# A graph network's sort of edges into slots: one of its three table operations goes from VectorE to GpSimd, and the scatter of edge weights is placed behind the sort

## The reference, cut to what matters

```python
def _L0_gnn_ref(feat, edge_src, edge_dst):
    deg = jax.ops.segment_sum(jnp.ones_like(edge_dst, dtype=feat.dtype), edge_dst, num_segments=n)
    norm = jnp.power(jnp.clip(deg, 1.0, None), -0.5)[:, None]
    for _ in range(10):
        msg = h[edge_src] * norm[edge_src]
        agg = jax.ops.segment_sum(msg, edge_dst, num_segments=n)
        h = 0.9 * (agg * norm) + 0.1 * feat_0
...
h = relu(layernorm(x)); x = x + _L0(h, src, dst)
h = relu(layernorm(x)); x = x + _L1(h, src, dst, q, k, v)             # attention over each node's edges
h = relu(layernorm(x)); x = x + _L2(h, edge_weight, W..., src, dst)   # weighted mean of neighbours
h = relu(layernorm(x)); x = x + _L3(h, ps_w, edge_attr_64, cj, ci, src, dst)  # edges weighed by a sigmoid
```

## Time and profile before

| | us |
|---|---|
| median of 3 runs | 1262.17 |
| the 3 runs | 1257.97, 1262.17, 1264.61 |
| the profiled execution | 1269.22 |
| its span, first to last instruction | 1267.4 |

### The profile page before, as it was taken

How to read it: one execution, slowest core, us unless ns; L and a number is a source line. 1 busy time by engine, 2 the same in 40 slices (tenths; PEclk the granted TensorE clock), 3 DMA queues, 4 the chain that set the end, 5 groups by cost and what they waited for, 6 DMA issues and landing times.

```text
span 1267.4 us, 32533 instructions
## 1 busy us (share of the span) xinstructions
PE 972.0 (77%) x12003; PEld 736.5 (58%) x12003; DVE 971.3 (77%) x1215; ACT 583.8 (46%) x1448; POOL 660.8 (52%) x446
## 2 busy tenths in 40 slices
PE   4967577785999999999993768778764776827774
PEld 3645456775454444444442668668764676727773
DVE  7988987888355555655446399999998699978996
ACT  1321027776011111111111377777774388938894
POOL 1006888888788788888878888898000000000000
PEclk9977776556999999999996588888897599968898
DMA  8652215554122222222403377787843878727784
GB/s 164 131 121 56 48 28 172 196 189 136 44 69 82 70 76 74 76 76 68 80 3 110 109 245 260 267 278 257 292 177 130 353 288 288 274 97 270 283 306 138
DMA packets 73563, 202.17 MB, mean 160 GB/s; under 512 B 36667, under 2 KB 37467, under 8 KB 73509
## 3 DMA queue, kind: packets, MB, share of 16 engines
q1 hardware_dynamic: 57300, 186.25, 41.6%
q10 hardware_dynamic: 2465, 13.60, 4.7%
q0 software_dynamic: 13744, 1.59, 4.0%
HBM read 155.30 MB, written 45.63 MB: 159 GB/s over the span
## 4 chain that ended last, share of the span: by engine, by line
PE 46%; DVE 26%; issue 15%; DMA 8%; ACT 2%; DVEq 1%; SPq 0%; another core or an unknown queue 0%; ACTq 0%
PE ps L1613 24%; DMA base_room<-ohd_table 5%; PE ps L1575 4%; PE ps L1473 4%; DVE arena L921 3%; PE ps L1430 3%; DVE arena L955 3%; DVE arena L909 3%; PE ps L1460 2%; PE ps L1415 2%; DVE arena L930 2%; DMA hl_room<-in_edge_attr_dram 2%; DVE arena L935 1%; DVE h_room L935 1%; PE ps L1378 1%
## 5 line engine op out<-in xcount | busy, mean ns | idle before, releaser
L558 POOL DMA_INDIRECT w_table<-wpa,slot_i x425 | 655.3, 1542 | 225.9 <-issue 225.9
L1613 PE MATMUL ps<-arena,hl_room 125*128 125x500 f16 (+1 forms) x1750 | 343.8, 352 | 11.2 <-DVEq L1197 10.5
L1415 PE MATMUL ps<-arena 125*128 125x64 f16 (+1 forms) x3900 | 235.8, 213 | 91.7 <-ACT arena L603 55.2
L1613 PEld LDWEIGHTS ps<-arena,hl_room 125*128 125x128 f16 x1750 | 155.5, 97 | 172.2 <-DVEq L1196 10.6
L1415 PEld LDWEIGHTS ps<-arena 125*128 125x128 bf16 x3900 | 182.3, 104 | 98.3 <-ACT arena L603 53.7
L682 ACT ACTIVATE part_room<-ps 128x500 f16<-128x500 f32 (+1 forms) x70 | 38.0, 543 | 320.1 <-PE ps L1613 207.5
L1205 DVE SCALAR_TENSOR_TENSOR part_room<-ps,part_room 128x500 f16<-128x500 f32 (+1 forms) x70 | 43.6, 622 | 158.8 <-ACT part_room L682 137.7
L603 ACT ACTIVATE arena<-ps 128x384 f32<-128x384 f32 x325 | 131.8, 505 | 13.2 <-PE ps L1420 8.1
L1420 PE MATMUL ps<-arena 125*128 (+1 forms) x1300 | 136.0, 205 | 0.0
L629 ACT ACTIVATE arena<-ps,part_room 128x64 f32<-128x64 f32 x500 | 107.4, 340 | 15.8 <-PE ps L1415 12.5
L1420 PEld LDWEIGHTS ps<-arena 125*128 125x128 bf16 x1300 | 114.3, 108 | 0.5
(11 more groups left out here) (261 smaller groups left out, 1454.8 us busy)
## 6 DMA issues: line engine op xcount, KB each, us to landing
hl_room<-slot_rows SPq DMA_DIRECT2D x49, 832.0 KB, 4.4
arena<-slot_rows SPq DMA_DIRECT2D x38, 832.0 KB, 15.8
arena<-ohd_table SPq DMA_DIRECT2D x26, 832.0 KB, 5.5
arena<-ohs_table SPq DMA_DIRECT2D x25, 832.0 KB
base_room<-ohd_table SPq DMA_DIRECT2D x24, 832.0 KB, 6.0
hl_room<-in_edge_attr_dram ACTq DMA_DIRECT2D x17, 750.0 KB
ohs_table<-xs_room SPq DMA_DIRECT2D x25, 448.0 KB
ohs_table<-xs_room SPq DMA_DIRECT2D x25, 384.0 KB
```

Source lines behind the costliest of these rows:

```text
L558: pool.indirect_dma_start(w_table, bass.IndirectOffsetOnAxis(slot_i[:, u:u + 1], 0), wpa[:, u], None).then_inc(S[f"w_out{g % 2}"], 16)
L1415: last = pe.matmul(ps[:, m % RING, o:o + b - a], slots[:, k * L:(k + 1) * L], rhs, start=(i == 0), stop=(i == 1))
L1613: last = pe.matmul(ps[:, c, 0:w], hl[0:P, u, s, :], adj[:, s, c * CH * P:c * CH * P + w], start=(s == 0), stop=(s == T - 1))
```

## The change

The product `to_col = hit_col * load_c` leaves VectorE's loop and is made by GpSimd, in a loop of its own that stands ahead of the scatters, behind a wait for the tables (`places_in`). GpSimd's product of tile t waits for the hits of tile t and for TensorE to have sorted tile t - 2, as VectorE's did. `hit_col` gets a second buffer, placed over `placed`, which has been read by then. VectorE's hits of tile t now wait for the product of tile t - 2, where they waited for that of t - 1 (the count of `to_slot` starts at 2 and not at 1, and TensorE's wait goes up by one with it). `per_edge` and `numbers` are the two views that were defined inside `sort_tile`, moved out. As GpSimd's queue is in order, all 425 scatters now stand behind the last product.

```diff
--- before.py
+++ after.py
@@ -182,6 +182,7 @@
         rank, over, tmp_j = cv([P, J]), cv([P, J]), cv([P, J])
         place = cv([P, J, 3])
         edge_i, first_t = cv([P, J], I32), cv([P, J])
+        placed_at = cv.at
         placed = cv([BT * JT, T // BT, P * 3])
         lane_c, col_c = cv([P, T, JP], F16), cv([P, T, JP], F16)
         load_i = cv([P, J], I32)
@@ -192,7 +193,8 @@
         to_lane_words, to_col_words = cv([P, 2, JP * L], BF16), cv([P, 2, JP * W2], BF16)
         to_lane = [to_lane_words[:, g].rearrange("p (a r b) -> p a r b", a=JP // 2, b=2) for g in range(2)]
         to_col = [to_col_words[:, g].rearrange("p (a r b) -> p a r b", a=JP // 2, b=2) for g in range(2)]
-        hit_col = cv([P, JP * W2], BF16).rearrange("p (a r b) -> p a r b", a=JP // 2, b=2)
+        hit_words = [cv([P, JP * W2], BF16), Carver(placed_at)([P, JP * W2], BF16)]
+        hit_col = [w.rearrange("p (a r b) -> p a r b", a=JP // 2, b=2) for w in hit_words]
         bits, bits_a = blank[:, 0:Q], blank[:, Q:2 * Q].bitcast(I32)
         bits_b = cv([L, Q], I32)
         sl, dl = cv([L, Q]), cv([L, Q])
@@ -255,6 +257,12 @@
         ohd2 = [w.rearrange("p (a r b) -> p a r b", a=CP, b=2) for w in ohd2_words]
         sums2 = cv([P, T, 2 * D])
         parts2 = cv([P, T, 2, D], F16)
+
+        def per_edge(tab, t, n):
+            return tab[:, bass.ds(t, 1), :].rearrange("p t (a b) -> p (t a) b", b=2).unsqueeze(2).to_broadcast([P, JP // 2, n, 2])
+
+        def numbers(n):
+            return rep2[0:P, 0:n, :].unsqueeze(1).to_broadcast([P, JP // 2, n, 2])
 
         def pairs(lanes, n):
             return lanes.rearrange("p (a b) -> p a b", b=2).unsqueeze(2).to_broadcast([L, n // 2, OW, 2])
@@ -543,6 +551,17 @@
                         pool.indirect_dma_start(rows[:, 0:D], None, g_table, bass.IndirectOffsetOnAxis(idx_s, 0)).then_inc(S[f"gathered{n // 2}"], 16)
 
             with pool.If(way < 1):
+
+                pool.wait_ge(S["places_in"], 1)
+
+                def column_loads(t, par):
+                    pool.wait_ge(S["hit_col"], t + 1)
+                    pool.wait_ge(S["sorted"], t + 1)
+                    pool.tensor_tensor(to_col[par], hit_col[par], per_edge(load_c, t, W2), ALU.mult).then_inc(S["to_slot"], 1)
+                with pool.Fori(0, T // 2) as i:
+                    for u in range(2):
+                        column_loads(i * 2 + u, u)
+                column_loads(T - 1, (T - 1) % 2)
 
                 pool.wait_ge(S["pa_ready"], 1)
                 pool.wait_ge(S["w_cleared"], 16)
@@ -1116,20 +1135,14 @@
                 fast(vec.tensor_copy(load_c[:, :, 0:JT], load_i.bitcast(F32).rearrange("p (t k) -> p t k", k=JT)))
                 vec.wait_ge(S["rep_ready"], 1)
 
+                vec.sem_inc(S["places_in"], 1)
+
                 def sort_tile(t, par):
-
-                    def over(tab, n):
-                        return tab[:, bass.ds(t, 1), :].rearrange("p t (a b) -> p (t a) b", b=2).unsqueeze(2).to_broadcast([P, JP // 2, n, 2])
-
-                    def numbers(n):
-                        return rep2[0:P, 0:n, :].unsqueeze(1).to_broadcast([P, JP // 2, n, 2])
                     vec.wait_ge(S["to_slot"], t + 1)
-                    vec.tensor_tensor(hit_col, numbers(W2), over(col_c, W2), ALU.is_equal).then_inc(S["hit_col"], 1)
+                    vec.tensor_tensor(hit_col[par], numbers(W2), per_edge(col_c, t, W2), ALU.is_equal).then_inc(S["hit_col"], 1)
                     vec.wait_ge(S["sorted"], t + 1)
-                    vec.tensor_tensor(to_lane[par], numbers(L), over(lane_c, L), ALU.is_equal).then_inc(S["to_lane"], 1)
-                    vec.wait_ge(S["hit_col"], t + 1)
-                    vec.tensor_tensor(to_col[par], hit_col, over(load_c, W2), ALU.mult).then_inc(S["to_slot"], 1)
-                vec.sem_inc(S["to_slot"], 1)
+                    vec.tensor_tensor(to_lane[par], numbers(L), per_edge(lane_c, t, L), ALU.is_equal).then_inc(S["to_lane"], 1)
+                vec.sem_inc(S["to_slot"], 2)
                 with vec.Fori(0, T // 2) as i:
                     for u in range(2):
                         sort_tile(i * 2 + u, u)
@@ -1521,7 +1534,7 @@
                 def sort_tile(t, par, early, late):
 
 
-                    pe.wait_ge(S["to_slot"], t + 2)
+                    pe.wait_ge(S["to_slot"], t + 3)
                     pe.wait_ge(S["to_lane"], t + 1)
                     for k in range(JT):
                         first, bank = early if k < JH else late
```

## The result

The changed kernel takes 1274.73 us in the median of 4 runs, the kernel before 1261.23 us in the median of 4: a ratio of 1.0101, 95% interval 1.0064 to 1.0137. It is slower, as forecast, but by 13 us and not by 37.

What follows compares the result with a forecast made beforehand. No engine was full, so the change was read in the sort, bound by VectorE: 25 tiles of 4.27 us plus 1.4 us make 108 us against 71.4. That +37 us on the 1262.17 us median gives 1299 us, range 1266 to 1327.

Steps and rivals of the forecast that it cites:

- The stage: The sort, VectorE's first column hit to its copy of the result: 71.4 us would become 108 us, +37 us.
- The engines exclude one another: In the sort, GpSimd stands still while VectorE streams two SBUF inputs, so products lie between VectorE's operations, not beside them.
- How they take turns: In the sort, VectorE runs two tiles ahead and stops; GpSimd then makes two products: 8.55 us a pair, 4.27 a tile.
- the other sign: Alternative sign of holding in the sort: longer hits and lane tables, instead of VectorE idle about 2 x 2.2 us every second tile.
- the price of product and hand-over: In the sort, per two tiles: two GpSimd products, 4.4 us, and two hand-overs of about 0.2 us each.
- The 0.08 us: In the sort, added to VectorE's 2 x 1.835 us for two tiles, giving 3.75 us.
- my bounds: GpSimd's product in the sort: 0.92 us for one stream, 1.76 for two inputs, 2.59 with output, 3.3 upper end.
- The hand-over: Passing between VectorE and GpSimd in the sort: about 0.2 us each, from the 0.16 us wait as nearest row.
- Waits for TensorE go inside: Three VectorE waits of 1.4 us for TensorE's edge work in the sort disappear inside the longer tiles.
- Scatters behind the sort: 32 delayed scatters: last begins at 979 us, table lands at 990, hidden by some 16 us; 0 in the sum.
- Side by side: Rival: in the sort, products run while VectorE streams; 2.3 us a tile, sort 60 us, 1251 us; chance 0.14, 0.10 faster.
- the forecast's own band: Held products of 1.1 to 3.3 us in the sort, giving 1271 to 1326 us; chance 0.72.

Runs made afterwards that it cites:

- the product alone: Changed kernel with VectorE made to wait for a tile's product before making that tile's lane table; 1299.09 us in one run, sort 100.9 us.
- the kernel that allows it: Changed kernel with the compared numbers of both hits and lane tables read from PSUM; ratio 0.9994 to the kernel before.
- the run that freed the hits alone: Changed kernel with only the hits' compared numbers read from PSUM, the lanes' left in SBUF; 1270.63 us in one run, sort 77.4 us.

## Why the prediction was right in sign and wrong in size

- **The stage.** Right: the loss lies between the first hits and the copy of the sorted sums, +14.0 us, where the medians differ by 13.5. The next stage is 6.5 us shorter in the profiled pair; whether it gives a part back regularly is open.
- **The engines exclude one another.** Right, and shown by taking one input after the other out of SBUF. The Trainium skill's rule (SBUF — State Buffer, Who interferes with whom), that the second to come waits for the whole of the first, agrees with the trace but for 0.15 us: the hits start 1.69 us before the product ends (115.97 and 117.66 us) and take 1.54 us more than alone.
- **How they take turns.** Wrong. I had read from the scatters that GpSimd gets in only when VectorE stops, so that products would come in pairs behind an idle VectorE. The product gets in at the seam of lane table and next hits, once a tile, and VectorE is never idle; only the long hits, which I had named as the other sign, show it. The reading of the earlier trace rows was at fault: the scatter's end lay behind the hole by chance of its length, and what releases it is the seam 1.14 us earlier.
- **The term of the sum that was mis-sized** is the price of product and hand-over. I took 2.2 us and 0.2 us a tile; measured are 1.55 us (1.75 alone) and nothing. The 0.08 us that I added for a pair of tiles are not there either. Of the 0.65 us between 2.2 and 1.55, 0.45 are a shorter product and 0.20 a part of it that holds nothing. 4.27 - 0.65 - 0.20 - 0.04 = 3.38 us, the measured tile. 25 x 0.89 = 22.3 us, and 1.5 us for the first hits, which nothing holds, less 1.0 us for the last wait (2.4 us, not 1.4), are the 22.8 us between the sort forecast (108.2 us) and measured (85.4). The product's own length stood among my bounds: two inputs read one after the other, 1.76 us from the slope of the earlier trace rows, against 1.75 us measured. I moved up from it by counting the output as a third stream, for which no row spoke. That the engine does read its inputs in turn is not shown by this agreement, and 1.76 us alone would still have given a sort of 97 us, 26 us more than before. The figure of the Trainium skill (GPSIMD Engine Reference, 3.1 Elementwise) would be an estimated 2.06 us; the measurement decides, and it is 1.75 us for bf16.
- **The hand-over** I priced by the 0.16 us of a semaphore. Such a hand-over does cost 0.14 to 0.19 us, as the product alone showed, but the one that matters here goes by no semaphore: in the changed kernel the product has started at 114.97 us, while the lane table runs to 116.05, and the hits have started at 115.97; each goes on when it is let in.
- **Waits for TensorE go inside.** Right: VectorE waits for none in the sort but the last 2.4 us.
- **Scatters behind the sort.** Right: hidden. The stretch of the earlier trace rows, which the prediction calls the first layer, lies in the attention layer; the sum does not hang on the name. The last one began at 983.49 us, where 979 on the old clock and 13.3 us for the later start of the decoding make 992; a landing of 8.2 us for 6.4, which the row transfers may explain; 10 and 14.5 us to spare in the two runs where I had 16.
- **The rivals.** Side by side did not happen here. In the kernel that allows it the sort took 65.9 us where the rival's price was 60, and that nearness is luck: its tile was put at 2.3 us and took 1.82, and the waits for TensorE were put at next to nothing and took 17.6. The product that held the sort (1.75 us alone) lies in the forecast's own band of 1.1 to 3.3 us, so the measured time lies near the lower end of the forecast's range, 1271 us; the range was right and the middle was not.

## What to carry to other kernels

Before work is moved from VectorE to GpSimd, count the inputs that VectorE's remaining operations have in SBUF: where they have two, GpSimd's time was added to VectorE's here, not laid beside it, so that 0.64 us taken off cost 1.55 us put on. One operand that never changes can be kept in PSUM instead, and here the two engines then ran side by side. When a stage gets faster, look at once for what was hidden in it: here the gain came only when TensorE's other work no longer stood in bundles.

## What the runs showed of the hardware that I had not expected

- A comparison of f16 numbers in PSUM with f16 in SBUF, written as bf16, was as fast as with both in SBUF: 1348 against 1346 ns for 125x2304, 635 against 646 ns for 125x936.
- An operation that was held took nothing beyond the wait: with the 1.55 us found in the run that freed the hits alone (2.82 - 1.27), the changed kernel's tile is 1.27 + 1.55 + 0.565 us, to 0.01 us.
- A scatter in the sort waits for one VectorE operation. In the attention layer it sat through two and more, with seams between them (844.16 us for one). Why it did not go on at the first seam there is open; nothing here tried it.
